# One transformer block with a routed feed-forward: the second norm's first half moved into the last attention turns, inverse roots of the later halves by Newton steps on VectorE

## What is computed

```
x  = _layernorm(hidden_states, ln1_g, ln1_b)
...
attn = jax.nn.softmax(scores, axis=-1)
ctx = jnp.einsum('bhst,bhtd->bhsd', attn, V)
attn_out = ctx @ out_U @ out_V + out_b
h = hidden_states + attn_out
x2 = _layernorm(h, ln2_g, ln2_b)
hmid = jax.nn.gelu(x2 @ fc1_U @ fc1_V + fc1_b, approximate=True)
mlp_out = hmid @ fc2_U @ fc2_V + fc2_b
return h + mlp_out
...
h = _layernorm(h + _L0_attn_ref(h, ...), axis=-1)
h = _layernorm(h + _L0_ffn_ref(h, ...), axis=-1)
```

## Time and profile before

| | us |
|---|---|
| median of 3 runs (227.41 to 229.1) | 227.68 |
| the profiled execution's time | 229.41 |
| its span, first to last instruction | 227.6 |
| TensorE busy | 214.5 (94%) |
| VectorE, ScalarE, GpSimd busy | 96.0, 93.6, 107.4 |
| mean granted TensorE clock | 0.981 of full speed |

### The profile page before, as it was taken

The page is one execution under the profiler, slowest core; times in us unless marked ns, Lnnn a source line. Parts: engine busy times, 40 slices in busy tenths (PEclk is TensorE's granted clock), DMA queues, the critical chain, the costliest instruction groups (busy, mean ns, idle before and its releaser), DMA issues.

```text
span 227.6 us, 4480 instructions
## 1 busy us (share of the span) xinstructions
PE 214.5 (94%) x1585; PEld 135.7 (60%) x1585; DVE 96.0 (42%) x262; ACT 93.6 (41%) x217; POOL 107.4 (47%) x149
## 2 busy tenths in 40 slices
PE   7999899888997999999999989999999999998992
PEld 4776577676784567766877733454443544434681
DVE  3165561868982320243689845221221212212044
ACT  2003645477674384454221432244433443334123
POOL 0030018487512399999970360555565564434000
PEclk9999999999998599999999999999999999999998
DMA  6999999200002991000110030298646232201552
GB/s 225 401 376 387 360 416 412 120 4 3 3 0 75 420 424 54 0 0 0 49 60 0 23 97 23 53 334 311 221 141 207 79 84 70 70 26 69 174 187 90
DMA packets 11647, 34.41 MB, mean 151 GB/s; under 512 B 2426, under 2 KB 4139, under 8 KB 11628
## 3 DMA queue, kind: packets, MB, share of 16 engines
q1 hardware_dynamic: 9612, 28.65, 33.7%
q0 software_dynamic: 2016, 5.51, 8.1%
HBM read 25.43 MB, written 4.01 MB: 129 GB/s over the span
## 4 chain that ended last, share of the span: by engine, by line
PE 82%; ACT 6%; DMA 5%; issue 3%; DVE 2%; POOL 1%; SPq 0%; ACTq 0%; POOLq 0%; DVEq 0%
PE ps L350 73%; PE ps L1673 3%; PE ps L1480 3%; DMA wres<-y_dram 3%; PE ps L1717 2%; ACT pair_mem L680 2%; ACT pair_mem L686 2%; DMA embed_sb<-embed 2%; DMA y_dram<-ln_mem,dest_i 1%; POOL y_dram L574 1%; ACT L605 1%; PE ps L1590 1%; PE ps L1359 0%; DVE ln_mem L878 0%; SPq L393 0%
## 5 line engine op out<-in xcount | busy, mean ns | idle before, releaser
L350 PE MATMUL ps<-wres,cT 128*64 (+1 forms) x360 | 68.1, 470 | 0.6 <-DVE cT L1266 0.6
L350 PEld LDWEIGHTS ps<-wres,cT 128*64 128x64 f32 (+1 forms) x360 | 24.8, 130 | 24.4 <-issue 16.5
L574 POOL DMA_INDIRECT y_dram<-ln_mem,dest_i x21 | 20.8, 988 | 35.0 <-ACT ln_mem L762 33.9
L1259 DVE TENSOR_TENSOR h<-ps,h 128x256 f32<-128x256 f32 x21 | 8.9, 425 | 54.2 <-ACT h L756 37.9
L565 POOL DMA_INDIRECT embed_sb<-x_dram,gather_i x21 | 20.7, 986 | 16.4 <-DVE gather_i L1191 10.3
L535 POOL TENSOR_SCALAR wres<-wres,mult 128x256 f32<-128x256 f32 x30 | 27.3, 923 | 0.0
L363 POOL TENSOR_TENSOR wres<-wres,cst_sb 128x148 f32<-128x148 f32 x24 | 10.9, 484 | 21.8 <-DVE wres L900 19.4
L756 ACT ACTIVATE h<-ps 128x256 f32<-128x256 f32 x21 | 8.1, 384 | 29.7 <-PE ps L350 25.9
L350 PE MATMUL ps<-h,stage 128*128 128x296 f32 x64 | 17.9, 419 | 0.0
L762 ACT ACTIVATE ln_mem<-ps 128x256 f32<-128x256 f32 x21 | 8.1, 384 | 19.4 <-PE ps L350 16.0
L1673 PEld LDWEIGHTS ps<-cst_sb,embed_sb 128*128 128x128 f32 x42 | 4.3, 141 | 16.4 <-issue 16.2
(11 more groups left out here) (201 smaller groups left out, 385.4 us busy)
## 6 DMA issues: line engine op xcount, KB each, us to landing
wres<-experts SPq DMA_DIRECT2D x15, 768.0 KB, 13.0
embed_sb<-embed SPq DMA_DIRECT2D x6, 416.0 KB, 5.3
wres<-ut SPq DMA_DIRECT2D x3, 768.0 KB, 9.0
stage<-shared SPq DMA_DIRECT2D x2, 771.0 KB, 13.5
wres<-y_dram SPq DMA_DIRECT2D x4, 384.0 KB, 4.9
stage<-wres SPq DMA_DIRECT2D x2, 512.0 KB
f1v<-fc_v SPq DMA_DIRECT2D x1, 512.0 KB
f2u<-fc_u SPq DMA_DIRECT2D x1, 512.0 KB
```

The costliest lines, as they stand in the source:

```text
L350: return nc.tensor.matmul(o, w, x, start=start, stop=stop)
L574: pool.indirect_dma_start(out=y_dram[:, :], out_offset=bass.IndirectOffsetOnAxis(ap=dest_i[:, column(i):column(i) + 1], axis=0), in_=ys[:, ...
L1259: nc.vector.tensor_tensor(a_r[:, i % 2], ps[:, 4 + i % 2, 0:F], gel_r[:, i % 2], ALU.mult).then_inc(a_done, 1)
```

## The change

It has four parts.

1. **The second norm's first half and its output projection move into turns 5, 6 and 7 of the attention.** `output_projection(0, 0)` stands in turn 5 and `output_projection(0, 1)` in turn 6 ahead of the probabilities times values; `attention_out(0)` at the head of VectorE's turn 6. The squares of this half are taken by GpSimd instead of ScalarE. In turn 7 `var(ln2, 0)` and `spread(ln2, 0)` stand on TensorE ahead of the probabilities times values, `std(ln2, 0)` on ScalarE behind the copies of the probabilities, and `inverse_std` and `scale` on VectorE ahead of the context. The second half's projections are placed among the first `hidden` steps (`OP_BANK` gives them banks 2 and 3).
2. **Gamma and beta of the second norm are folded into the MLP's first weights.** GpSimd multiplies `f1u` by gamma; TensorE multiplies the unscaled `f1u` by beta (two matmuls of one column, ahead of turn 0), ScalarE copies the result to `z_b`, and `z1_out` adds it. The four `affine_act` instructions of this norm go, and `first_low` reads the scaled rows.
3. **`inverse_root` on VectorE takes the place of Sqrt and reciprocal** in norm 2's second half and both halves of norm 3: 13 instructions on 74 columns, each waiting for the one before. Two Gelu and Sqrt table changes go on ScalarE with the Sqrts.
4. **Norm 3 and the routing are placed anew.** The eight `keep_clock` matmuls go; `spread(ln3, 0)` stands ahead of the last `second_low`; `mlp_out(1)` between gate and input of unit 0; `var(ln3, 1)` behind unit 1; `spread(ln3, 1)` and `logits` behind unit 2's matmuls. Each step of `routing` stands one unit later, and `slot_table` behind unit 7's matmuls.

```
-OP_BANK = (0, 4)
+OP_BANK = (0, 2)
...
@@ POOL
             over_pairs(pool.Fori, turn)
+            pool.wait_ge(cmp_mm, 5)
+            for c in range(DC):
+                pool.tensor_scalar(f1u[:, c], f1u[:, c], vec[:, C_LN2G + c:C_LN2G + c + 1], None, ALU.mult) \
+                    .then_inc(f1u_done, 1)
+            for c in range(DC):
+                pool.wait_ge(op_done, c + 1)
+                nc.gpsimd.tensor_tensor(sq[:, 0, c], h1[:, c, 0:HT], h1[:, c, 0:HT], ALU.mult).then_inc(ln2.sq, 1)
@@ ACT turn
+                if ahead == 0:
+                    std(ln2, 0)
                 if not (isinstance(p, int) and p == 0):
                     context_out(p - 1)
@@ ACT
-            squares(ln2, 0, half(h1, 0), op_done, True)
-            std(ln2, 0)
+            warm(ACT.Gelu_apprx_tanh)
             context_out(PAIRS - 1)
-            affine_act(ln2, 0, C_LN2G, C_LN2B)
-            squares(ln2, 1, half(h1, 1), op_done, True)
-            std(ln2, 1)
-            warm(ACT.Gelu_apprx_tanh)
...
+                if g == 1:
+                    squares(ln2, 1, half(h1, 1), op_done, True)
+                if g == 11:
                     squares(ln3, 0, half(hs, 0), mo_done, True)
-            std(ln3, 0)
+            warm(ACT.Gelu)
             squares(ln3, 1, half(hs, 1), mo_done, True)
-            std(ln3, 1)
-            warm(ACT.Gelu)
@@ DVE
+            def inverse_root(ln, n):
+                y, t = nw[:, 1], nw[:, 2]
+                dve.wait_ge(ln.var, n + 1)
+                var = ps[:, ln.banks[n], VAR:VAR + QT]
+                step(nc.vector.tensor_scalar(t, var, EPS, None, ALU.add))
+                step(nc.vector.tensor_scalar(nw_i[:, :], t.bitcast(I32), 1, None, ALU.arith_shift_right))
+                step(nc.vector.tensor_scalar(y.bitcast(I32), nw_i[:, :], -1.0, float(0x5f3759df), ALU.mult, ALU.add))
+                step(nc.vector.tensor_scalar(nw[:, 0], t, -0.5, None, ALU.mult))
+                for k in range(NEWTON):
+                    step(nc.vector.tensor_tensor(t, y, y, ALU.mult))
+                    step(nc.vector.tensor_tensor(t, t, nw[:, 0], ALU.mult))
+                    last = nc.vector.scalar_tensor_tensor(rs[:, n] if k == NEWTON - 1 else y, t, 1.5, y, ALU.add, ALU.mult)
...
             z1_out(0)
-            inverse_std(ln2, 1)
+            attention_out(1)
+            inverse_root(ln2, 1)
             scale(ln2, 1, half(h1, 1))
...
             mlp_out(0)
-            z2_out(1)
-            inverse_std(ln3, 0)
-            mlp_out(1)
+            inverse_root(ln3, 0)
             scale_h3(0)
-            inverse_std(ln3, 1)
-            scale_h3(1)
+            z2_out(1)
+            mlp_out(1)
             def routing(k):
+                if k == 0:
+                    inverse_root(ln3, 1)
                 if k == 1:
+                    scale_h3(1)
+                if k == 2:
                     select()
...
-                if k == 6:
+                if k == 7:
                     owners()
                     tables()
@@ PE
+            for c in range(DC):
+                last = mm(ps[:, 7, 0:1], f1u[:, c], vec[:, C_LN2B + c:C_LN2B + c + 1], c == 0, c == DC - 1)
...
             for g in range(2, NH * FIC):
-                hidden(g)
+                if g != FIC:
+                    hidden(g)
                 second_low(g - 2)
-                if g == 5:
+                if g == FIC:
+                    hidden(g)
+                if g == 3:
+                    var(ln2, 1)
+                if g == 6:
+                    spread(ln2, 1)
+                if g == 7:
                     first_low(1)
                 if g == 10:
                     mlp_out(0)
-                if g == 13:
+                if g == 12:
                     var(ln3, 0)
             second_low(NH * FIC - 2)
+            spread(ln3, 0)
             second_low(NH * FIC - 1)
-            keep_clock(1, 4)
-            mlp_out(1)
-            spread(ln3, 0)
-            keep_clock(7, 4)
...
-                    if k == 1 and which:
-                        spread(ln3, 1)
+                    if k == 0 and which:
+                        mlp_out(1)
-                if k == 0:
+                if k == 1:
                     var(ln3, 1)
-                if k == 1:
+                if k == 2:
+                    spread(ln3, 1)
                     logits()
```

More of the change, by code:

```diff
@@ L954, in turn @@
             def turn(p, par, ahead):
+                if ahead == 1:
+                    attention_out(0)
+                if ahead == 0:
+                    inverse_std(ln2, 0)
+                    scale(ln2, 0, half(h1, 0))
                 if ahead >= 3:
@@ L968, in turn @@
                     sums(p + 1, 1 - par)
-                if ahead == 1:
-                    attention_out(0)
             over_pairs(dve.Fori, turn)
-            inverse_std(ln2, 0)
-            scale(ln2, 0, half(h1, 0))
-            attention_out(1)
             def mlp_out(n):
@@ L1499, in turn @@
                     scores(p + 2, par)
+                if ahead == 2:
+                    pe.wait_ge(ct_done, PAIRS // 2)
+                    pe.wait_ge(s_cen, PAIRS - 1)
+                    output_projection(0, 0)
                 if ahead == 1:
-                    pe.wait_ge(ct_done, PAIRS // 2)
-                    output_projection(0, 0)
+                    output_projection(0, 1)
+                if ahead == 0:
+                    var(ln2, 0)
+                    spread(ln2, 0)
+                if isinstance(p, int) and p == 0:
+                    pe.wait_ge(cmp_done, 5)
                 pe.wait_ge(v_done, p + 1)
@@ L1513, in turn @@
                 last.then_inc(pv_mm, 1)
-                if ahead == 1:
-                    output_projection(0, 1)
             over_pairs(pe.Fori, turn)
-            var(ln2, 0)
-            context_transposed(PAIRS - 1)
-            pe.wait_ge(ct_done, PAIRS)
-            output_projection(1, 0)
-            spread(ln2, 0)
-            output_projection(1, 1)
             def first_low(n):
-                pe.wait_ge(ln2.aff, DC * (n + 1))
+                pe.wait_ge(f1u_done, DC)
+                pe.wait_ge(ln2.out, DC * (n + 1))
                 for k in range(DC):
-                    last = mm(ps[:, n, 0:HT], f1u[:, k], xn[:, k, n * HT:(n + 1) * HT], k == 0, k == DC - 1)
+                    last = mm(ps[:, n, 0:HT], f1u[:, k], sq[:, n, k], k == 0, k == DC - 1)
                 last.then_inc(z1_mm, 1)
```

70 lines of the change are left out of this document (45 added, 25 removed).

## The result

The changed kernel takes 249.28 us, median of 4 runs (247.92 to 251.45), beside 228.39 for the kernel before (227.41 to 232.49, 4 runs): a ratio of 1.0943, 95% interval [1.0884, 1.1002]. Single times and medians are of all executions, the ratios and their intervals of the fast ones alone, since in some executions of every kernel the time is some per cent longer. The kernel is slower, as forecast, but by some 21 us instead of 7, far above the range. The profiled execution took 247.92, with a span of 246.1 where before had 227.6, and a mean granted clock of 0.951 where before had 0.981.

A forecast was written before the change was run, and what follows sets the result against it. TensorE, 82% of the chain of waits, was taken to bound the kernel. Terms + 0.2 + 0.15 + 3.9 + 1.9 - 1.6 = + 4.5 on 227.6 gave 232.1; one more clock fall, 2.5, gave 234.6, forecast 234.7, range 227.0 to 238.5.

The forecast's parts named there:

- the price of a root: VectorE's 13 chained instructions per inverse root, in norms 2 and 3, take 3.7 us beside GpSimd's work.
- the quiet price: A root on VectorE without GpSimd's work beside it: 13 x 0.26 = 3.4 us.
- The step that failed next: the clock: TensorE's clock falls behind turn 7 as before, and once more at the logits or first tiles, costing 2.5 us.
- part 4's saving of 1.6: Between norm 3 and unit 0 on TensorE the filler matmuls go, saving 1.6 us.
- Turn 7: In the last attention turn TensorE waits 1.4, 0.3 and 0.45 us; total 2.2 against 2.0, a loss of 0.2.
- Part 2: Folding gamma and beta: two one-column matmuls and ScalarE's copy ahead of turn 0 cost 0.15 us (0 to 0.4).
- Norm 2's wait: Ahead of the spread of norm 2's second half, TensorE waits 0.8 us for the root.
- Norm 3's: TensorE waits for the roots of norm 3: 0.3 us at its first half, 1.8 at its second.
- The logits: Directly behind norm 3's last spread, the logits wait 1.0 us more for the scaled rows.
- The gather: Routing ends a unit later, so TensorE waits 1.9 us (1.7 to 2.8) for the first gathered tile.
- ScalarE's table load: Ahead of turn 7's copies of the probabilities, the load takes 1.28 us; the next activation starts 1.30 behind its start.
- the first rival: The clock holds in the last turns and behind, only the waits are paid: 228.7 us, chance 0.10.

The follow-up runs named there:

- A: The changed kernel, with all four parts of the change: 249.28 us.
- A with fillers: A with bf16 matmuls on zeros ahead of the three spreads, the logits and the first gathered tile: 241.97 and 243.06 us.
- GpSimd still, with fillers: A with GpSimd idle during the roots (experts' factors left out) and fillers of 3, 10, 7 and 16 matmuls in the waits: 235.67 us.
- the mended kernel: A with the root's estimate in PSUM, logits and first transposes inside unit 3, owners' instructions behind unit 6's routing step, fillers of 12 and 5: 230.90 us.
- B: The kernel before the change: 228.39 us.
- y in PSUM: A with the root's estimate y kept in PSUM, so each two-input instruction reads one input from there: 237.80 us.

## Why the prediction was wrong, and where it was right

**Where the loss lies.** Of the 16.55 us in the stretch: 8.0 are the clock (A less A with fillers), 6.8 GpSimd's hold on VectorE (that less GpSimd still, with fillers), 2.3 the last placing and the fall of 3.4 us behind turn 7 that the mended kernel did not have (74.17 less 71.84); that makes 17.1, and the mended kernel's stretch is 0.5 under B's. These are differences of single profiled stretches, and fillers that shorten as the roots do, so their parts hold to about 1 us and not to tenths. Outside it, 0.6 us lie ahead of turn 5, and 1.4 behind the first tile (96.76 instead of 95.41), where the clock is at half speed for 3.4 us.

**The step that failed first: the price of a root.** The direction was right, and so were the places where TensorE waits; the sizes were not. For a root I took 3.7 us, from eight VectorE instructions beside GpSimd averaged to 0.32 each; they took 5.3 to 6.5. In the forecast's sum the new waits made 3.9 us; measured they are 3.46, 2.08, 3.27 and 0.94, together 9.75. The average was over unlike things. The eight are of 15 and 75 columns, and one, of 0.23, reads PSUM; two products of 75 columns, both with all operands in SBUF, take 0.44 and 0.24 (at 117.16). A root has 12 of its 13 instructions with all operands in SBUF. Two of the eight:

```profile
116.41 0.23 DVE L1116 SCALAR_TENSOR_TENSOR jump<-ps,over 128x75 f32<-128x75 f32 x1
116.68 0.44 DVE L1121 TENSOR_TENSOR slot<-slot,jump 128x75 f32<-128x75 f32 x1
```

My upper bound of 4.2 left out also that the first root's neighbours on GpSimd would be casts and subtractions, which hold to their end. Even so, the quiet price was right to 0.02 us (3.4 against 3.38).

The trace shows a hold up to the end of GpSimd's cast or subtraction, and none for an instruction that reads one input from PSUM. The Trainium skill, page "SBUF — State Buffer", section "Who interferes with whom", states this rule: a VectorE instruction with two SBUF inputs contends with a GpSimd instruction that reads SBUF, one with at most one SBUF input and outside the two-port modes does not, and the lock is exclusive, for the two-port modes over the whole instruction. The runs here agree on who is held. A hold over the whole instruction they show for casts and subtractions, not for the multiplications, 0.92 us each, beside which VectorE's instructions take 0.24 to 0.60. In norm 3's first root, for one, each of the last four that are held ends 0.55 or 0.56 us behind the start of a multiplication, and what follows inside the same multiplication takes 0.24. The prediction named the price of a quiet instruction only; this rule, which speaks against the edit, was the one to weigh.

**The step that failed next: the clock.** I had it fall behind turn 7, as before, and once more at a cost of 2.5 us. It held behind turn 7 with 2.04 us of waits (my 2.2), and fell at all four long waits, 23.9 us at half speed. I had counted with waits of 1.8 and 1.9 us and one fall between them; the waits were 2.1 to 3.5 us, each brought a fall, and of these one was half as long again as the 6.7 us that I priced a fall by, 10.2, one as long, 6.8, and two half as long, 3.4. On the span the change costs 18.5 us where I had 7.0. The waits of the roots and logits account for 5.9 of the difference, part 2 and the gather for 0.6; with part 4's saving of 1.6 taken as forecast, about 5 are left for the clock, which then cost some 7.7 in place of 2.5, close to the 8.0 of the fillers run. The single fall in the earlier trace rows was weak ground for a rule, since other executions of the same kernel, by their mean clock, don't have it.

**Point by point.** Turn 7: forecast 1.4, 0.3 and 0.45, measured 1.10, 0.42 and 0.52. Part 2: forecast 0.15, up to 0.4; the two one-column products leave four records of 0.61 us in all on TensorE's path, and the way from the embedding to turn 5 is 0.5 longer. The weight loads of these four records, 128x128 each, take 0.52 of it in the trace. Norm 2's wait: 0.8 forecast, 3.46 measured. Norm 3's: 0.3 and 1.8 forecast, 2.08 and 3.27 measured. The logits: 1.0 and 0.94. The gather: 1.9 and 2.14. ScalarE's table load: 1.28 us, and the next activation 1.29 behind its start, with no further cost, as I had it from the earlier trace rows. With y in PSUM the last wait, 2.05 us, is near the forecast's 1.8: the scheme of "root less the matmuls in between" was sound, and the root's size was off.

**The rivals.** None covered this. The clock held in the last turns, as the first rival had it, and the time still came out highest of all, for the falls moved to the longer waits.

## What to carry to other kernels

Before a chain of short VectorE instructions is put on the critical path, look at what GpSimd does in that very stretch, and at where each operand lies: one operand in PSUM took the hold away, and 11.5 us with it. Price such a chain by the rows of its own kind of instruction, not by an average over a mixed group. A wait costs more than its length once the clock goes with it, here some 8 us beside 11.9 us of new waits, and it can be won back with fillers only where a fall does come.

## What the runs showed that I had not expected

- VectorE's 74-column products with both inputs in SBUF take 0.24 us with GpSimd still and up to 1.20 beside a GpSimd subtraction of 96x512, ending 0.09 us behind it; with one input in PSUM 0.23 or 0.24 beside the multiplications, and 0.23 the one time that it stood beside a cast.
- An in-SBUF `tensor_scalar` of one input is held too: 0.53 and 0.59 instead of 0.20. The same operation with its output in PSUM took 0.24.
- Two one-column fp32 matmuls cost TensorE 0.61 us for their four records.
- The half-speed stretches up to the first tiles and among the last sums measured 3.4, 6.8 or 10.2 us in every profile here.
- The 24 embedding matmuls at the start take 11.91 to 13.61 us in different executions of the same instructions; what sets it was not looked into.
- Whether GpSimd's multiplications could be given another place at no cost to the gather or the experts was not tried.
